# Query projection of a perceiver block: four weight-block sums moved to GpSimd, and one panel's products reordered

## What is computed

```python
q  = layernorm(x) @ Wq + bq          # 512 rows, 1024 x 1024 weights
kv = ctx_2048 @ Wkv + bkv            # 8192 rows, 1024 x 2048 weights
k, v = split(kv)                     # then quantised, attended, projected
```

## Time and profile before

| | |
|---|---|
| median of three runs | 2580.9 us (2578.14 to 2580.93) |
| the profiled execution, its own time | 2579.91 us |
| its span, first to last instruction | 2578.1 us |
| TensorE busy | 2393.7 us, 93% |
| VectorE busy | 1934.8 us, 75% |
| ScalarE busy | 1403.1 us, 54% |
| GpSimd busy | 883.5 us, 34% |
| mean granted TensorE clock | 0.986 of full |

### The profile page before, as it was taken

One profiled execution on the slowest core, in us unless ns is written; L12 is line 12 of the kernel. 1 busy time (PEld: TensorE's weight loads), 2 busy tenths in 40 slices (PEclk: granted clock), 3 DMA queues, 4 the chain that ended last, 5 costly groups with the idle time before them and its releaser, 6 DMA issues. The chain is left out here.

```text
span 2578.1 us, 44284 instructions
## 1 busy us (share of the span) xinstructions
PE 2393.7 (93%) x15976; PEld 1221.2 (47%) x15976; DVE 1934.8 (75%) x2964; ACT 1403.1 (54%) x2131; POOL 883.5 (34%) x433
## 2 busy tenths in 40 slices
PE   6999999999999999999778888888879998999998
PEld 3444444444444444444345555555555466444444
DVE  8977677767676767767799999999986446566664
ACT  5345555554555455554289999999983146111101
POOL 0423332233223322332176566575652551011100
PEclk9999999999999999999989999999999998999999
DMA  6144444444444444444579999999983340000000
GB/s 270 50 115 112 107 122 121 115 106 122 117 119 107 121 122 112 116 114 114 155 170 217 220 205 210 225 200 214 212 211 131 131 101 17 1 17 17 1 5 33
DMA packets 553654, 320.55 MB, mean 124 GB/s; under 512 B 397888, under 2 KB 529216, under 8 KB 548288
## 3 DMA queue, kind: packets, MB, share of 16 engines
q1 hardware_dynamic: 553536, 318.87, 48.7%
HBM read 149.95 MB, written 69.21 MB: 85 GB/s over the span
## 5 line engine op out<-in xcount | busy, mean ns | idle before, releaser
L1731 DVE TENSOR_SCALAR_CACHE_REDUCE at_sc<-at_score 128x1024 f32<-128x1024 f32 x512 | 597.2, 1220 | 16.7 <-PE at_score L1560 12.0
L1833 ACT ACTIVATE at_sc<-at_sc,at_bias,at_qs 128x4096 uint16<-128x4096 f32 x128 | 486.2, 3798 | 20.5 <-DVE at_bias L1743 20.0
L1327 POOL TENSOR_TENSOR wt_stage<-wt_stage,kv_bias 128x1024 f32<-128x1024 f32 x64 | 173.9, 2717 | 727.0 <-DVE wt_stage L1114 727.0
L1019 ACT ACTIVATE wt_stage<-wt_stage,kv_magic,kv_inv 128x64 f32<-128x64 f32 x960 | 324.5, 426 | 112.5 <-DVE kv_inv L1142 75.4
L1149 DVE SCALAR_TENSOR_TENSOR wt_stage<-wt_stage,kv_sc 128x1024 f32<-128x1024 f32 x60 | 74.0, 1234 | 219.0 <-ACT wt_stage L1019 219.0
L1560 PE MATMUL at_score<-x,at_q 128*128 128x512 f16 x512 | 158.5, 393 | 67.4 <-DVE at_sc L1731 47.9
L1001 ACT ACTIVATE q_t<-q_t 128x512 f16<-128x512 f32 x128 | 79.5, 622 | 230.5 <-PE kv_kz L936 118.1
L1560 PE MATMUL at_score<-wt_stage,at_q 128*128 128x512 f16 x512 | 154.7, 384 | 52.4 <-DVE at_sc L1731 45.1
L1516 POOL TENSOR_TENSOR wt_stage<-wt_stage,at_vi 128x2048 f32<-128x2048 f32 x32 | 145.5, 4546 | 130.5 <-DMA wt_stage<-values 130.5
L936 PE MATMUL kv_ky<-kv_units,q_t 128*128 128x512 f16 x768 | 176.2, 379 | 0.0
L936 PE MATMUL kv_vy<-kv_units,q_t 128*128 128x512 f16 x756 | 173.8, 380 | 0.0
(11 more groups left out here) (344 smaller groups left out, 4612.5 us busy)
## 6 DMA issues: line engine op xcount, KB each, us to landing
kv_rows<-in_ctx SPq DMA_DIRECT2D x64, 512.0 KB, 6.6
values<-wt_stage SPq DMA_DIRECT2D x32, 1024.0 KB, 6.6
keys_turned<-o SPq DMA_DIRECT2D x32, 1024.0 KB, 5.2
wt_stage<-values SPq DMA_DIRECT2D x16, 2048.0 KB, 8.7
wt_stage<-keys_turned SPq DMA_DIRECT2D x32, 512.0 KB, 5.2
x<-keys_turned SPq DMA_DIRECT2D x31, 512.0 KB, 5.2
x<-in_x SPq DMA_DIRECT2D x2, 2048.0 KB, 8.2
kv_units<-in_wq SPq DMA_DIRECT2D x2, 2048.0 KB, 12.7
```

The lines of the kernel that those rows point to most:

```text
L1019: last = nc.scalar.activation(key[:, s, cols], key[:, s, cols], ACT.Identity, bias=magic[:], scale=inv[:, h:h + 1])
L1327: nc.gpsimd.tensor_tensor(key[:, s, :], key[:, s, :], bias[:, 0:D], ALU.add).then_inc(key_biased, 1)
L1731: nc.vector.tensor_scalar(sc[n % 2][:, c * SC:(c + 1) * SC], score[pos % 2][:], 1.0, None, ALU.mult, ALU.max, accum_out=part_max[n % 2][:, ...
L1833: nc.scalar.activation(prob[n % 2][e], sc[n % 2][:, e * EC:(e + 1) * EC], ACT.Exp, bias=bias[n % 2][:], scale=qs_pair[j][:, t:t + 1], accu ...
```

## The change

The four sums T1 and T3 of `vw` and `kw` are taken out of VectorE's list and put on GpSimd, which runs them one after the other in the order T1 of `vw`, T1 of `kw`, T3 of `vw`, T3 of `kw`, with the same waits for the loads, and behind a wait for the normalised rows (T1 overwrites x). T2 stays on VectorE.

TensorE makes the products of the first panel in another order: for all four tiles first the high by high and low by high products, which need the panel's high part alone, and only then, behind the wait for its low part, the high by low products. The second panel is as before. The number of products is the same.

```diff
+        @block.gpsimd
+        def _(pool):
+            pool.wait_ge(turner.rows_ready, (turner.norms + 1) * T)
+            vw.sum_t1(pool)
+            kw.sum_t1(pool)
+            vw.sum_t3(pool)
+            kw.sum_t3(pool)
...
             vw.low(dve, vw.B11)
             kw.low(dve, kw.B11)
-            vw.sum_t1(dve)
-            kw.sum_t1(dve)
             vw.low(dve, vw.B22)
             vw.low(dve, vw.B21)
-            vw.sum_t3(dve)
             vw.sum_t2(dve)
             kw.low(dve, kw.B22)
             kw.low(dve, kw.B21)
-            kw.sum_t3(dve)
             kw.sum_t2(dve)
...
             turner.tensor(pe)
-            for n in range(2):
-                w_hi, w_lo = panels.parts[n]
-                pe.wait_ge(panels.lo_ready, n + 1)
-                for t in range(T):
-                    if n == 0:
-                        turner.wait_tile(pe, t)
...
+            w_hi, w_lo = panels.parts[0]
+            pe.wait_ge(panels.hi_ready, 1)
+            for t in range(T):
+                turner.wait_tile(pe, t)
+                tok = slice(t * P, (t + 1) * P)
+                for k in range(KD):
+                    for a in (turner.xt_hi, turner.xt_lo):
+                        nc.tensor.matmul(acc[t][:], a[:, k, tok], w_hi[:, k, :], start=(k == 0 and a is turner.xt_hi),
+                                         stop=False)
+            pe.wait_ge(panels.lo_ready, 1)
+            for t in range(T):
+                tok = slice(t * P, (t + 1) * P)
+                for k in range(KD):
+                    last = nc.tensor.matmul(acc[t][:], turner.xt_hi[:, k, tok], w_lo[:, k, :], start=False,
+                                            stop=(k == KD - 1))
+                last.then_inc(panels.summed, 1)
+            w_hi, w_lo = panels.parts[1]
+            pe.wait_ge(panels.lo_ready, 2)
...
-    def sum_t1(self, dve):
-        dve.wait_ge(self.loaded["b11"], 16)
-        dve.wait_ge(self.loaded["b12"], 2 * 16)
-        self.nc.vector.tensor_tensor(self.t1, self.b12, self.b11, ALU.subtract).then_inc(self.summed, 1)
+    def sum_t1(self, pool):
+        pool.wait_ge(self.loaded["b11"], 16)
+        pool.wait_ge(self.loaded["b12"], 2 * 16)
+        self.nc.gpsimd.tensor_tensor(self.t1, self.b12, self.b11, ALU.subtract).then_inc(self.summed, 1)
```

More of the change, by code:

```diff
@@ new lines, in _ @@
+            w_hi, w_lo = panels.parts[1]
+            pe.wait_ge(panels.lo_ready, 2)
+            for t in range(T):
+                pe.wait_ge(turner.lo_ready, turner.first + len(turner.units))
+                tok = slice(t * P, (t + 1) * P)
+                for k in range(KD):
+                    for p, (a, b) in enumerate(((turner.xt_hi, w_hi), (turner.xt_hi, w_lo), (turner.xt_lo, w_hi))):
+                        last = nc.tensor.matmul(acc[T + t][:], a[:, k, tok], b[:, k, :],
+                                                start=(k == 0 and p == 0), stop=(k == KD - 1 and p == 2))
+                last.then_inc(panels.summed, 1)
@@ L713, in low, with sum_t3 @@
                                             op1=ALU.subtract).then_inc(self.lo_ready, 1)
-    def sum_t1(self, dve):
-        dve.wait_ge(self.loaded["b11"], 16)
-        dve.wait_ge(self.loaded["b12"], 2 * 16)
-        self.nc.vector.tensor_tensor(self.t1, self.b12, self.b11, ALU.subtract).then_inc(self.summed, 1)
[L720 to L723, removed]
+    def sum_t1(self, pool):
+        pool.wait_ge(self.loaded["b11"], 16)
+        pool.wait_ge(self.loaded["b12"], 2 * 16)
+        self.nc.gpsimd.tensor_tensor(self.t1, self.b12, self.b11, ALU.subtract).then_inc(self.summed, 1)
+    def sum_t3(self, pool):
+        pool.wait_ge(self.loaded["b22"], self.rest)
+        pool.wait_ge(self.summed, 1)
+        self.nc.gpsimd.tensor_tensor(self.b12, self.b22, self.b12, ALU.subtract).then_inc(self.summed, 1)
     def sum_t2(self, dve):
```

## The result

The changed kernel takes 2590.3 us (median of nine runs, 2587.06 to 2591.91), the kernel before 2580.93 us beside it (nine runs). The medians are 9.4 us apart. The ratio of the runs is 1.0034 with a 95% interval of 1.0024 to 1.0043, which makes the change 8.8 us slower, between 6.2 and 11.1. The sum of the prediction had 2587.4 us on the profiled execution and 2588.4 on the median.

A forecast was written before the change was run, and what follows sets the result against it. Two nearly equal chains, PE's and DVE's, bound the block. Four GpSimd sums (+4 x 4.4), less 4 x 2.2 on VectorE and 1.3 us, give +7.5, with 0 behind the barrier: 2579.9 + 7.5 = 2587.4 us, range 2582.5 to 2591.5.

The forecast's parts named there:

- The sum of the prediction: Whole kernel: 2579.9 us profiled plus 7.5 us gives 2587.4 us; 2588.4 us on the median of the runs.
- What bounds: In the block, PE's and DVE's chains are nearly equally long; shortening one alone brings 0.2 us.
- TensorE: In the block, products follow the transposes without a wait and end at 63.8 us instead of 72.6.
- The price of an add on GpSimd: Beside VectorE instructions with two SBUF inputs, engines take turns; each sum costs 4.4 us, between 4.3 and 4.55.
- The order of the steps: In the block, VectorE gets one instruction between every two GpSimd adds; POOL is done at 60.70 us, the last query at 80.9.
- the sum by balance: For the block: +4 x 4.4, -4 x 2.2, less 1.3 us of old gaps and hidden starts, giving +7.5 us.
- Behind the barrier: After the block, all engines start 7.5 us later; PE's clock effects, between +1.2 and -1.7 us, taken as 0.
- rival B: Behind the barrier, no clock fall at 98 us and one fewer later, 1.7 us each: 2584.0 us; chance 12%.
- Rival C: Behind the barrier, PE's half-clock start isn't hidden because DVE waits for PE sooner: 3.4 us more, 2590.8 us; chance 8%.
- Rival A: In the block, POOL's adds run beside DVE without taking turns: -4.0 us, 2575.9 us; chance 10%.
- The rule of the Trainium skill: VectorE and GpSimd contend when VectorE has two SBUF inputs, no size given; freshly loaded code's first call pays about 6 us.

The follow-up runs named there:

- e1: The kernel before with only TensorE's new order, all sums staying on VectorE: ratio to before 1.0000 (0.9990 to 1.0009).
- e5: The changed kernel with GpSimd waiting for the end of each add before the next: ratio to before 1.0032 (1.0022 to 1.0043).
- e8: The changed kernel run once more, unaltered, on the same chip as the others: ratio to before 1.0035 (1.0022 to 1.0048).
- e2: The changed kernel with TensorE's old order, so only the four sums move to GpSimd: ratio to before 1.0037 (1.0022 to 1.0051).
- e3: The changed kernel with T3 of both weights back on VectorE, T1 of both on GpSimd: ratio to before 1.0016 (1.0006 to 1.0026).
- e6: The kernel before with T4 of `vw` moved from VectorE's next block to GpSimd beside the eight query instructions: ratio 0.9993; repeated with more runs, 0.9988.
- e4: The kernel before with TensorE's new order, T1 and T3 on VectorE made for one column of 2048 only: ratio 0.9976, 6.3 us faster.

## Why the prediction was right

- **What bounds.** Right. Two chains of nearly equal length, and with PE's shortened by 8.5 us the end didn't move (e1).
- **TensorE.** Right in each term: products from 22.57 us, no wait at the panel's low part, 0.216 us each (the first 64 in 13.81 us) at a granted clock of 1.00, end at 64.17 us against the 63.8 of the working.
- **The price of an add on GpSimd.** Right in kind, a little low in size: 4.4 us was taken between 4.3 and 4.55, and the adds behind one another show 4.5 (47.95 to 52.46, and 4.54 for the last). From 37.01 us, where VectorE's last free instruction ends, to 57.00 us VectorE got one instruction of 2.14 us, so the four adds held it for 17.85 us against the 17.6 of the sum. That is 0.25 of the 0.33 us between the 7.5 forecast and the 7.83 of the chain; the rest is in what was set against them, about 1.2 us instead of 1.3. The nearest row was the add of the same size beside PSUM readers, and the slope from the shorter ones was the weaker guide.
- **The order of the steps.** Wrong in one place. The working gave VectorE one instruction between every two adds, ending at 60.7 us for POOL; in the trace POOL ran three adds in a row and was done at 57.00 us, and `vw.low(B22)` was held 13.4 us. It changed nothing in the sum, since VectorE had only such instructions to run, and e5, where the turns are as forecast, ends within 0.29 us. The prediction had the sum by balance as well, which is why the step didn't matter.
- **Behind the barrier.** 0 was taken between +1.2 and -1.7 us. In the trace the delay of 7.83 us had shrunk to 7.0 us at the attention (both counted from L285), so 0.8 us came back. PE started at half clock, which cost about 1.4 us (8 products in 3.17 us) and filled its old wait of 2.2 us (0.7 us of it is left). The fall of the clock at 98 us, worth about as much, is gone, as rival B had it, and PE's waits for VectorE up to 205 us are 2.6 us in all instead of 3.2. So the two ends of the clock's account cancelled, as the sum had assumed, and of B's 3.4 us only these 0.8 came. Rival C didn't come: VectorE didn't wait for PE sooner.
- **Behind the attention's start.** The prediction put nothing there. The runs are 8.8 us slower by the ratio, against 7.4 us between the two starts of the attention. The interval of the ratio holds both, so this is no error shown, but it isn't shown to be noise either (see e8).
- **Rival A** fell with e2 and e3, and its other half, free adds beside PSUM readers, stood in e6. Its working also had the point that `vw.sum_t2` waits for GpSimd even with free adds; e4 shows that at no cost at all the gain would be 6.3 us, so even the best case for the change was smaller than the 8.8 us it took from VectorE's list.
- **The rule of the Trainium skill.** The Trainium skill, "GPSIMD Engine Reference", section "Key points", names contention where VectorE has two SBUF inputs; the traces agree in where it falls (e6 against e2) and put a size to it, the whole length of the add. In the same page the section "Instruction dispatch" has about 6 us for the first call of a freshly loaded kernel; it did not show: the first add began at 36.62 us, when its load had landed, and ran 4.78 us, 0.39 us of it behind DVE's instruction that ended at 37.01.

## What to carry to other kernels

Before work is moved to GpSimd, look at what VectorE runs beside it: next to instructions with two SBUF inputs an add costs VectorE its full time on GpSimd, here twice the time saved, while beside VectorE's eight instructions with one input in PSUM and one in SBUF it was free in four traces. Add the two engines' own times and compare with the old chain; where VectorE has only instructions of the first kind to run, the order of turns need not be known. And where two chains end together, an engine that is made early alone gains nothing and may start the next stage at half clock.

## What the runs showed that I had not expected

GpSimd doesn't always give way to a waiting VectorE instruction between two of its own, even to one that was there first. With adds issued back to back, VectorE got in behind the first of four (41.40 us) but not behind the second and third, and one instruction of 2.28 us stood for 15.68 us; the same in e2 (15.69) and e8 (15.68). With a wait for its own end between adds (e5) GpSimd gave way each time. But the wait isn't needed for it. In e3, with two adds and none of such waits, VectorE got in between them (its two instructions end at 45.61 and 52.27 us, 2.15 us behind each add). In the trace of before, the code has such a wait between L1313 and L1317 but none behind L1317, where L1098 got in the earlier trace rows, and none between the adds of L612, where L285 got in the earlier trace rows. What decides it is open: I tried only the wait.
